# One decoder layer on one core: the values' projection stands earlier in a step, and VectorE adds a variance's constant ahead of a mask

## What is computed

```python
x = _layernorm(x + _L0_attn_ref(x, L0_attn_qkv_weights), axis=-1)
x = _layernorm(x + _L0_xattn_ref(x, ctx_1024, ctx_1024, Wq, Wk, Wv), axis=-1)
x = _layernorm(x + _L0_ffn_ref(x, gate_w, gate_b, sw1, sb1, sw2, sb2, rw1, rb1, rw2, rb2), axis=-1)
```

## Time and profile before

| | |
|---|---|
| median of 3 runs | 726.83 us (725.86 to 726.84) |
| the profiled execution | 727.77 us, span 725.6 us |
| busy share of the span | PE 94%, PEld 81%, DVE 67%, ACT 66%, POOL 47% |
| main stage's steps 66.6 to 368 us | one step about every 11.1 us |
| granted clock of PE over the span | 0.986 |

### The profile page before, as it was taken

One profiled execution on the slowest core, in us unless ns is written; L12 is line 12 of the kernel. 1 busy time (PEld: TensorE's weight loads), 2 busy tenths in 40 slices (PEclk: granted clock), 3 DMA queues, 4 the chain that ended last, 5 costly groups with the idle time before them and its releaser, 6 DMA issues.

```text
span 725.6 us, 21537 instructions
## 1 busy us (share of the span) xinstructions
PE 682.8 (94%) x6174; PEld 589.5 (81%) x6175; DVE 489.3 (67%) x1563; ACT 478.6 (66%) x1319; POOL 341.7 (47%) x467
## 2 busy tenths in 40 slices
PE   7979999899999999999998889889999999999994
PEld 6868888788888888888887655779999999998653
DVE  3666877598888888888887456445555555555266
ACT  0278888588888888888885141356766666666246
POOL 1001334235454454554545446045656655556395
PEclk9999999899999999999999899999999999999998
DMA  8634469522332232323325224687777777776597
GB/s 314 216 131 138 140 198 308 194 61 76 91 94 70 89 100 75 107 80 107 112 80 173 76 72 147 186 220 132 139 133 142 135 139 134 141 135 133 118 349 264
DMA packets 93915, 104.30 MB, mean 144 GB/s; under 512 B 13168, under 2 KB 86640, under 8 KB 92944
## 3 DMA queue, kind: packets, MB, share of 16 engines
q1 hardware_dynamic: 78480, 79.43, 36.8%
q0 software_dynamic: 14656, 23.26, 16.8%
q10 hardware_dynamic: 704, 0.66, 0.3%
HBM read 62.21 MB, written 41.10 MB: 142 GB/s over the span
## 4 chain that ended last, share of the span: by engine, by line
PE 76%; DMA 6%; DVE 5%; SPq 4%; POOL 4%; issue 4%; ACT 1%; DVEq 0%; POOLq 0%; ACTq 0%
PE ps L1038 15%; PE ps L1047 8%; PE ps L803 6%; PE ps L902 5%; PE ps L791 5%; PE ps L768 4%; PE ps L813 4%; PE ps L905 4%; PE ps L735 4%; PE ps L926 4%; PE ps L771 4%; POOL first_use L711 2%; DMA xg<-sent 2%; PE ps L1025 2%; PE ps L823 2%
## 5 line engine op out<-in xcount | busy, mean ns | idle before, releaser
L1105 ACT ACTIVATE prob<-ps,nmax 128x128 f32<-128x128 f32 x512 | 146.5, 378 | 28.0 <-DVE nmax L1319 28.0
L1038 PEld LDWEIGHTS ps<-xgT,attn_only 128*128 128x128 f32 x1136 | 135.9, 192 | 7.4 <-DVE ghT L1600 1.8
L1038 PE MATMUL ps<-xgT,attn_only 128*128 128x128 f32 x1136 | 138.9, 276 | 1.1 <-ACT xgT L1217 1.1
L670 POOL DMA_INDIRECT total<-rot,result_row x71 | 112.4, 1583 | 35.3 <-issue 32.9
L1319 DVE TENSOR_REDUCE nmax<-ps 128x4 f32<-128x512 f32 x128 | 82.1, 685 | 17.9 <-PE ps L791 17.3
L1600 DVE SCALAR_TENSOR_TENSOR ghT<-ps,attn_only 128x128 f32<-128x128 f32 x142 | 43.3, 346 | 69.5 <-PE ps L1038 58.1
L613 POOL TENSOR_TENSOR rot<-products 128x128 f32<-128x128 f32 x128 | 61.1, 498 | 61.6 <-DVE products L1329 61.5
L1112 ACT COPY pT<-ps 128x512 f32<-128x512 f32 x124 | 74.3, 599 | 19.6 <-PE ps L803 15.3
L803 PE MATMUL ps<-tf,prob 128*128 128x128 f32 x512 | 78.5, 276 | 5.2 <-DVE pT L1434 4.2
L637 POOL DMA_INDIRECT sent<-packets,pos x64 | 63.4, 990 | 36.8 <-PE ps L791 22.6
L1047 PE MATMUL ps<-first_use,ghT 128*128 x284 | 74.5, 385 | 0.0
(11 more groups left out here) (143 smaller groups left out, 1407.0 us busy)
## 6 DMA issues: line engine op xcount, KB each, us to landing
xg<-sent SPq DMA_DIRECT2D x71, 130.5 KB, 2.1
attn_only<-in_L_ffn_rb SPq DMA_DIRECT2D x71, 130.0 KB
first_use<-total SPq DMA_DIRECT2D x12, 512.0 KB, 8.5
total<-zeros POOLq DMA_DIRECT2D x1, 4224.0 KB, 18.0
k_dram<-first_use SPq DMA_DIRECT2D x4, 1024.0 KB, 5.1
attn_only<-in_x_turned SPq DMA_DIRECT2D x32, 128.0 KB, 2.3
attn_only<-k_dram SPq DMA_DIRECT2D x256, 16.0 KB
attn_only<-in_x SPq DMA_DIRECT2D x32, 128.0 KB, 2.7
```

The source lines that it names most:

```text
L670: eng.indirect_dma_start(totals[slot % 2], bass.IndirectOffsetOnAxis(ap=result_row[:, slot:slot + 1], axis=0), yw[:, slot, :], None, compu ...
L1038: mm = eng.matmul(ps[:, 2 * r + half, f * P:(f + 1) * P], w_now[:, r, c, cols:cols + P], xgT[:, r, c, :], start=(c == 0), stop=(c == DC - 1))
L1105: ins = eng.activation(prob[:, t % 2, 4 * u + n, :], SCORE[u][:, n * P:(n + 1) * P], ACT.Exp, bias=nmax[:, t % 2, 4 * u + n:4 * u + n + 1])
```

## The change

`project(t)` is split in two. `project_values(t)`, the two matmuls into columns 256 to 511, is called between the third turn of the probabilities (behind the second attention's scores SCX) and the transposes of x2; from t = 4 on it waits for `pq_set` of that step, which counts VectorE's reading of the turned queries in the same bank. `project_queries(t)` stays in the old place and counts `qv_made`. On VectorE `add_eps` of the second variance now stands ahead of `lay_mask(n+1, 3)`. No instruction is added or removed.

```diff
--- before.py
+++ after.py
@@ -754,22 +754,24 @@
             eng.wait_ge(small_in, 64)
             eng.wait_ge(consts_set, 2)
 
-            def project(t):
+            def project_values(t):
 
                 eng.wait_ge(xT_in[t % 2], t // 2 * 16 + 16)
                 if t < 4:
                     after(eng, q_set, t)
                     after(eng, v_set, t)
-                if t == 4:
-                    eng.wait_ge(pq_set, 2)
+                else:
+                    eng.wait_ge(pq_set, 2 * (t - 4) + 2)
+                for c in range(DC):
+                    eng.matmul(QV[:, D:2 * D], xT[:, t % 2, c, :], wqkv_sb[:, c, 2 * D:3 * D],
+                               start=(c == 0), stop=(c == DC - 1))
+
+            def project_queries(t):
                 after(eng, res2_set, t - 4)
                 for m in range(DC):
                     for c in range(DC):
-                        eng.matmul(QV[:, m * P:(m + 1) * P], wqkv_sb[:, c, m * P:(m + 1) * P], xT[:, t % 2, c, :],
-                                   start=(c == 0), stop=(c == DC - 1))
-                for c in range(DC):
-                    mm = eng.matmul(QV[:, D:2 * D], xT[:, t % 2, c, :], wqkv_sb[:, c, 2 * D:3 * D],
-                                    start=(c == 0), stop=(c == DC - 1))
+                        mm = eng.matmul(QV[:, m * P:(m + 1) * P], wqkv_sb[:, c, m * P:(m + 1) * P], xT[:, t % 2, c, :],
+                                        start=(c == 0), stop=(c == DC - 1))
                 mm.then_inc(qv_made, 1)
 
             def lay_first_masks():
@@ -941,6 +943,8 @@
                 shared_between(n)
                 if live(n - 1):
                     turn_probs(n - 1, 2)
+                if live(n + 1):
+                    project_values(n + 1)
                 t = n - 5
                 if live(t):
 
@@ -972,7 +976,7 @@
                         mm = eng.matmul(GATE, x2T[:, t % 2, c, :], gate_w_sb[:, c, :], start=(c == 0), stop=(c == DC - 1))
                     mm.then_inc(gate_made, 1)
                 if live(n + 1):
-                    project(n + 1)
+                    project_queries(n + 1)
                 if n == 0:
                     eng.wait_ge(kk_set, 12)
                     project_k(NG - 1, 1, 5)
@@ -1531,10 +1535,9 @@
                     lay_mask(n + 1, 0)
                 if live(t4):
                     aggregate(t4, bn2, mv2, bn2_set, mv2_set)
+                    add_eps(t4, mv2, mv2_set)
                 if live(n) and live(n + 1) and n > 0:
                     lay_mask(n + 1, 3)
-                if live(t4):
-                    add_eps(t4, mv2, mv2_set)
                 if live(t4):
                     eng.wait_ge(rstd2_set, t4 + 1)
                     after(eng, sent_in[t4 % SLOTS], t4 // SLOTS * 32)
```

## The result

The changed kernel takes 736.76 us (median of 6 runs, 734.57 to 742.52); the kernel before, run beside it, 726.71 (725.86 to 728.68). The ratio is 1.0136, 95% interval 1.011 to 1.0162: **slower**, as forecast, and 0.3 us from the forecast time. The profiled execution took 734.57 us, where the forecast in its own terms was 738.1.

The account below looks back on a forecast made before the run. It took a chain of PE (94% busy) and VectorE, through YX, res2 to gc and turned x1, as the bound. Terms 11.3 - 0.6 - 0.4 + 0 = +10.3 us on 726.8 gave 737.1 us; own range 735 to 740.5, 8-in-10 range 731 to 740.5.

Parts of the forecast that it names:

- The mechanism: Steady step: moved values delay YX, then res2 to gc takes 2.04 us, so PE idles 0.61 ahead of turned x1.
- The price of a step: Steps n = 4 to 30: each 0.42 us longer, 27 of them, +11.3 us.
- The early term: Steps n = 1 and 3, without YX: values fit into PE's waits, 0.3 us gained each, -0.6 us.
- The stretch n = 8 to 9: PE's 2.9 us wait for a context transfer: one step's 0.42 us vanishes in it, -0.4 us.
- The constant: VectorE's 0.15 us instruction ahead of the last cast: packets' wait goes, later cast holds nothing up, 0 us.
- ScalarE's 0.10 of slack: ScalarE ahead of x1T: of 0.36 us of idle, 0.10 is left after the change.
- its queries hold the scores: End of PE's chain in a step: scores start 0.16 us behind the queries that ScalarE scales.
- Rival A: PE's hole is simply filled, turned x1 not waiting for gc or gc coming sooner: 721.1 us, chance 0.09.
- rival B: The moved values' wait for pq_set costs nothing, steps 0.20 us longer: 731.2 us, chance 0.09.
- D: Whole kernel: gains and losses cancel, time within 0.2% of 726.8 us, chance 0.05.
- Rival C: PE's clock falls to half rate after idling, in five steps, 10 us more: 747 us, chance 0.04.
- 0.26 us of slack: Steady step before the change: PE's turned x1 could start about 308.43, waiting on gc, but PE arrives at 308.69.

Follow-up runs that it names:

- e3: Changed kernel with VectorE's mean and variance of res1 and its constant ahead of res2: 727.90 us, 1.0003 to the kernel before.
- e13: Kernel before with VectorE's x1 and gc ahead of the statistics of res2: 725.94 us, 0.9995 to the kernel before.
- e1: Changed kernel with VectorE's constant back behind the last cast, so only the values moved: 737.46 us, 1.0132 to the kernel before.
- e14: Kernel before with the values moved only in steps n up to 3: 725.88 us, 0.9988 to the kernel before.
- e2: Kernel before with only VectorE's constant moved ahead of the last cast: 727.40 us, 0.9994 to the kernel before.
- e9: Kernel before with ScalarE copying turned x1 only after its mask and scaled queries: 731.75 us, 0.9991 to the kernel before.
- e4: Changed kernel run once more, nothing altered: 735.46 us, 1.0097 to the kernel before.
- e11: Changed kernel, VectorE's res1 mean and variance before res2, x1 and gc before res2's statistics, ScalarE's x1T and x2T copies later: 726.60 us, 0.9902 to before.
- e16: The kernel of e11 run once more, nothing altered: 721.62 us, 0.9929 to the kernel before.

## Why the prediction was right, point by point

- **The mechanism** held at each link, in rows: the values 0.14 behind the second product (0.15), res2 0.63 behind YX (0.63), 2.04 to gc's end (2.04), turned x1 at 0.15 (0.14), PE idle ahead of it for 0.61 (312.18 + 0.97 = 313.15 to 313.76; 0.61). e3 shows the causal part: 0.29 us off VectorE's piece took 0.29 off the step; e13 shows that before it took nothing.
- **The price of a step** was mis-sized: 0.48, not 0.42. Values behind a wait take 0.94 to the next matmul (309.78 to 310.72), not the 0.87 of the earlier trace rows, where their first weights had been loaded beside the matmul ahead; that is the 0.07 of the difference, less small parts. So 27 plain steps would cost 13.0, not 11.3. e1 excludes the constant. That the weights' first row leads the matmul's by 0.11 us before and by 0.03 behind the wait (L771, L766) fits this.
- **The early term** was 0.90, not 0.6 (e14), against a trace in which the clock held; against the four others of that early order it would be 2.3 to 2.5.
- **The stretch n = 8 to 9** was put at 0.4 given back. Its two steps should add 1.0, and it took 2.7 less: 3.7. This is the term that was furthest off. The forecast let the transfers swallow a step's price; that part came to 0.8. The other 2.9 is the granted clock, 0.88 before and 1.00 changed, which this term did not have.
- **Sum**: from the start of YX in n = 4 the parts are +1.4, -2.7, +9.2, -0.2 and -0.9, with +0.3 ahead: +7.1, the difference of the spans. (The 0.3 holds YX's own delay in n = 4, the early gain and a later start of the stage; the 0.9 lies behind n = 35 and was in no term.) The forecast has +10.3 for this pair. The medians differ by 10.1, the profiled execution being the fastest of its six, and by 8.2 in the second set. That the forecast met the first median within 0.3 us is luck; that the kernel is slower, by 5 to 12 us over the two intervals, is not.
- **The constant** at 0 was right in PE's old order (e2) and 0.35 us off in the new one (e1); the masks were laid at 315.08, 0.46 ahead of the scores.
- **ScalarE's 0.10 of slack** was wrong, 0.29 (e3); it didn't matter for the forecast. So was the claim that its queries hold the scores (e9).
- **Rival A** fell with the row of gc, rival B with the 0.14, D with the ratio. Rival C named the right thing with the wrong sign. The clock did cost 3.1 us in the drain in one of two traces (e4), but on average it was higher in the changed kernel than before (0.991 to 0.986, e4).

The wait for pq_set, 0.2 us of the price, is there because the turned queries and the values share bank 6, not a column. The Trainium skill (PSUM — Partial Sum Buffer, PSUM bank collisions raise a hardware error) asks to keep engines apart by bank, not by address; no run here tried without.

## What to carry to other kernels

Work that fills a hole on the busiest engine may already be the cover of another wait: before moving it, add up what the other engine needs from the point that the move delays to the point that waits for it, and compare it with what is left between them. The same edit (two small instructions ahead of res2) was worth -0.29 and +0.33 us a step in two orders of the program; what decides is whether the engine idles at that place. A wait listed at 17 us may be worth nothing, and a wait that isn't listed (0.26 us of slack) may decide. Before two traces are compared stretch by stretch, look at the granted clock of each stretch: here it made a difference of 2.9 us that no wait explains.

## What the runs showed of the hardware that was not expected

- One program, one wait of 1.44 us on PE, two outcomes: clock at 1.00, or an average of 0.86 for 12 us, 3.1 us in all (e4).
- In n = 10 to 30, where the profile gives PE no wait over 0.45 us, the clock was 1.00 in all thirteen traces. Up to n = 35 it fell only at three places, each with waits of 0.9 to 3.3 us: before n = 4, in n = 8 to 10 and in the drain. The same order of instructions gave a fall in one execution and none in another (the changed kernel and e4; e11 and e16).
- The plain steps of one order repeat to 0.01 us over most executions (before, e1, e9 and e13 show some of 0.03 to 0.08 more, and before one of 0.2, n = 18), while times of one kernel differ by up to 8 us; the steps are the better instrument here.
- The values' matmuls behind a wait cost 0.07 us more than in a stream, and PE's weight loads idle 0.2 us between the weighing and the scores with nothing to wait for (e9).
